# A graph network kernel: GpSimd waits for four gathers to land before it issues the next four

## The chip, the cores and the metric

The kernel runs on one core of a Trainium2 chip. The metric is the device time of one execution in microseconds, from the first to the last instruction and what lies around them; lower is better.

## The reference: what is computed

There are 6,250 nodes of 160 numbers (64 scalars, 32 vectors of three) and 206,250 edges, sorted by destination. Two layers follow each other, each with a residual and a layer norm:

```
layer 0:  message = (products of x[src] with weights, scaled by the edge's 4 numbers)
                    * sigmoid(edge_scalars @ W_rad.T + b_rad)
          x = layernorm(x + linear(x + segment_sum(message, dst)))
layer 1:  w   = silu(edge_scalars @ Wfc1) @ Wfc2
          mid = w * (linear(x)[src] combined with the edge's 4 numbers)
          x = layernorm(x + sc(x) + alpha * linear(segment_mean(mid, dst)))
```

The costly part of each layer is the same: fetch one row per edge from a table of node rows in HBM, weight it by the edge's numbers, and sum the rows of equal destination.

## The kernel before

**Tiles.** 128 edges are a tile, four tiles a supertile (512 edges), four supertiles a round. There are 404 supertiles, that is 101 rounds, in each layer. The node rows are multiplied by the weights once, ahead of the edges, and stored in HBM as `table0` (448 floats, 1,792 bytes a row) and `table1` (224 floats, 896 bytes a row).

**Gathers.** GpSimd (POOL) fetches rows with indirect DMAs, 128 rows each, so four for a supertile (`gather`, line 361): 1,616 in each layer. The rows of a supertile go to one of four slots, `rows0[:, j]` or `rows1[:, j]`, with j the supertile's place in its round. Each slot has a semaphore, `s_rows[l][j]`, which the DMA engines raise by 16 for each landed gather, so by 64 for a supertile. Before GpSimd issues the gathers of slot j again, it waits until ScalarE (`s_wtd`) and VectorE (`s_wone`) have read the rows of four supertiles ago, and at slot 0 also for the row numbers of this round (`s_src`, the buffer `srcs`). It never waits for its own gathers. The first 16 gathers of a layer are issued before the loop, with no wait between them.

**The other engines.** For each supertile of layer 0, ScalarE weights the rows by three of the edge's numbers (line 433) and takes the sigmoid (line 459). VectorE adds finished sums of two supertiles ago (line 668), weights by the fourth number (line 609), makes the one-hot matrices of the destinations (line 660), sums the parts (line 625) and makes the messages (line 632). TensorE makes the radial product of the supertile after the next (line 883) and the sums of this one (line 907). Layer 1 is alike: lines 433 and 517 on ScalarE, 668, 612, 660 and 645 to 655 on VectorE, 900, 892 and 907 on TensorE. The order is written out by hand, and each engine runs its own loop over the rounds.

**Loads by SP.** SyncE (SP) loads the edge scalars and destinations of two supertiles at a time into buffers that are used again each round, and after them the row numbers for the round after the next (line 270). That load is issued only when all gathers that used the buffer have landed.

Of the kernel before, what the change touches and what calls it, by code (L numbers as in the profile page):

```python
# [11 lines left out]
TPS = 4  # L12
SUP_EDGES = TPS * P
SLOTS = 4
# [33 lines left out]
def mk_gnn_resnorm_d2_gnn_r8_694f30_kernel(nc, a):  # L48
# [5 lines left out]
    with ctx:  # L54
# [3 lines left out]
        def sem(name):  # L58
            return ctx.enter_context(nc.semaphore(name))
# [117 lines left out]
        s_rows = [[sem(f"rows_gathered{l}_{j}") for j in range(SLOTS)] for l in range(2)]  # L177
        s_pool, s_sp = sem("pool_went_on"), sem("sp_went_on")
# [157 lines left out]
        @block.gpsimd  # L336
        def _(pool):
            pool.dma_start(dsts, a["dsts"]).then_inc(s_dsts, 16)
            for t, name in WEIGHTS:
                pool.dma_start(t[:], a[name]).then_inc(s_weights, 16)  # L340
            nc.gpsimd.memset(zeros[:], 0.0).then_inc(s_const, 1)
            nc.gpsimd.memset(eps[:], EPS).then_inc(s_eps, 1)
            nc.gpsimd.memset(ident[:], 0.0).then_inc(s_const, 1)
            pool.wait_ge(s_const, 2)
            nc.gpsimd.affine_select(out=ident[:], in_=ident[:], compare_op=ALU.not_equal, fill=1.0, base=0,
                                    pattern=[[-1, P]], channel_multiplier=1).then_inc(s_const, 1)
            nc.gpsimd.memset(msg0[:, :, :, DIM:MSG0], 1.0).then_inc(s_zero0, 1)
            nc.gpsimd.memset(acc0[:, :, DIM:MSG0], 0.0).then_inc(s_zero0, 1)

            pool.wait_ge(s_ends, 2)  # L350
            for e in range(2):
                pool.dma_start(wends_d[e:e + 1, :].rearrange("o (p s) -> (o p) s", s=SLOTS),
                               wends[:, e, :]).then_inc(s_endsout, 16)
            pool.wait_ge(s_endsout, 32)
            pool.dma_start(wtabf[:, 0:2, :], wends_d.rearrange("(o e) s -> o e s", o=1)).then_inc(s_endsin, 16)
            nc.gpsimd.iota(iota[:], pattern=[[1, NODES_PAD]], base=0, channel_multiplier=0).then_inc(s_const, 1)

            def gather(l, j, b):
                rows, table = (rows0, table0) if l == 0 else (rows1, table1)
                for t in range(TPS):  # L360
                    pool.indirect_dma_start(  # L361
                        out=rows[:, j, t, :], out_offset=None, in_=table,
                        in_offset=bass.IndirectOffsetOnAxis(ap=srcs[:, b, j, t:t + 1], axis=0)).then_inc(s_rows[l][j], 16)

            def gathers(l):
                pool.wait_ge(s_src[l][0], 16)
                for j in range(SLOTS):
                    gather(l, j, 0)

                def gathers_of_round(r, b, loads):  # L370
                    for j in range(SLOTS):
                        s = (r - 1) * SLOTS + j
                        pool.wait_ge(s_wtd[l], s + 1)
                        pool.sem_inc(s_pool, 1)
                        pool.wait_ge(s_wone[l], s + 1)
                        pool.sem_inc(s_pool, 1)
                        if j == 0:
                            pool.wait_ge(s_src[l][b], loads * 16)
                            pool.sem_inc(s_pool, 1)
                        gather(l, j, b)  # L380

                with pool.Fori(0, TWOS) as i:
                    gathers_of_round(i * 2 + 1, 1, i + 1)
                    gathers_of_round(i * 2 + 2, 0, i + 2)

            for j in range(GROUP):
                pool.wait_ge(s_tst[j], 16 * GROUPS)
            pool.wait_ge(s_wtab, 1)
            gathers(0)

            pool.wait_ge(s_done[0], 1)
            nc.gpsimd.memset(tails[:, NODE_TILES * MV:], 0.0).then_inc(s_tails, 1)
            nc.gpsimd.tensor_copy(tails[:, 0:NODE_TILES * MV].rearrange("p (w c) -> p w c", w=NODE_TILES),
                                  acc0[:, :, P:DIM]).then_inc(s_tails, 1)
            nc.gpsimd.memset(og_tail[:, :, GROUP * MV:], 0.0).then_inc(s_pad, 1)
            nc.gpsimd.memset(arena[:, 0:KEPT0], 0.0).then_inc(s_zero1, 1)
            nc.gpsimd.memset(arena[:, KEPT1:], 0.0).then_inc(s_zero1, 1)

            for g in range(GROUPS):
                pool.wait_ge(s_fev, (g + 1) * GROUP)  # L400
                pool.wait_ge(s_ln[0], (g + 1) * LN_STEPS[0])
                to, f = acc0[:, g * GROUP:(g + 1) * GROUP, :], feat[:, g % 2]
                nc.gpsimd.tensor_tensor(to[:, :, 0:P], f[:, :, 0:P], og[:, g % 2], ALU.add)
                nc.gpsimd.tensor_tensor(to[:, :, P:DIM], f[:, :, P + ROW1:],
                                        og_tail[:, g % 2, 0:GROUP * MV].rearrange("p (g c) -> p g c", g=GROUP),
                                        ALU.add).then_inc(s_base, 1)

            for b in range(2):
                pool.wait_ge(s_fst[b], (GROUPS + 1 - b) // 2 * 16)
            pool.wait_ge(s_base, GROUPS)  # L410
            gathers(1)
# [753 lines left out]
```

## Time and profile before

| what | us |
|---|---|
| median of 3 runs | 5922.7 |
| lowest and highest | 5918.03, 5962.53 |
| span of the profiled execution, first to last instruction | 5900.5 |
| busy: TensorE, VectorE, ScalarE, GpSimd | 3955.8, 3891.0, 3383.0, 3146.9 |

The list of times does not say which of them is the profiled execution; the lowest is 17.5 us above its span. A share of busy time is an average over the whole span. The indirect DMA's busy time on GpSimd is the time in which it writes the descriptors; the bytes move behind it, and where they do can be read from the share and rate of the DMA engines in short stretches. Layer 0 gathers from 66 us to 2860 us and layer 1 from 2993 us to 5801 us. The granted TensorE clock is 0.5 of full speed in most of layer 0 and mostly full in layer 1.

### The profile page before, as it was taken

What the parts mean: (1) busy time and instruction counts of PE and PEld (TensorE: products, weight loads), DVE (VectorE), ACT (ScalarE), POOL (GpSimd) and SP (SyncE); (2) the same over time, 40 slices, a digit from 0 to 9 for tenths busy, and PEclk for the clock granted to TensorE, in tenths of its full rate; (3) what the DMA queues carried; (4) which work ended last, traced back from release to release, by engine and by line L of the source; (5) the groups of instructions that cost most, each with busy time, mean ns of one, the idle gap of its engine ahead of it and who ended that gap; (6) DMA issues with size and microseconds to landing.
All of it is one profiled execution on the core that took longest, in us unless ns stands there. A gap on an engine that the chain in (4) does not pass through costs nothing.

```text
span 5900.5 us, 82997 instructions
## 1 busy us (share of the span) xinstructions
PE 3955.8 (67%) x16478; PEld 2613.9 (44%) x16479; DVE 3891.0 (66%) x12732; ACT 3383.0 (57%) x10841; POOL 3146.9 (53%) x3275
## 2 busy tenths in 40 slices
PE   5555555555565565565667777778777777777776
PEld 3444444444444444454544343434434334344345
DVE  4666666666666666666656666667666666666666
ACT  3556655655655565665555565555555555555554
POOL 4555555555555555555345555555555555555551
PEclk7555555555555555555688888888888888888888
DMA  7555555555555555555332222222222222222222
GB/s 232 140 142 143 141 145 139 141 144 139 141 145 140 138 146 139 139 145 142 90 81 75 74 75 74 78 73 77 75 74 75 73 72 75 73 76 77 74 76 53
DMA packets 325631, 641.98 MB, mean 109 GB/s; under 512 B 143598, under 2 KB 175131, under 8 KB 325499
## 3 DMA queue, kind: packets, MB, share of 16 engines
q0 software_dynamic: 181584, 557.89, 34.8%
q1 hardware_dynamic: 144016, 83.72, 5.4%
q8 instruction: 14, 0.23, 0.0%
q14 instruction: 17, 0.14, 0.0%
HBM read 620.47 MB, written 20.88 MB: 109 GB/s over the span
## 4 chain that ended last, share of the span: by engine, by line
DVE 34%; another core or an unknown queue 23%; PE 22%; issue 12%; DVEq 4%; ACT 3%; DMA 1%; POOL 0%; SPq 0%; ACTq 0%
PE ps L907 15%; DVE work L625 10%; DVE onehot L660 7%; DVE work L609 5%; ACT work L433 3%; PE ps L900 3%; DVE work L612 2%; PE ps L892 2%; DVEq L676 2%; DVE work L648 2%; DVE dstf L704 1%; DVEq L721 1%; DVE work L655 1%; DVE acc L668 1%
## 5 line engine op out<-in xcount | busy, mean ns | idle before, releaser
L361 POOL DMA_INDIRECT arena<-table,srcs x1616 | 1541.1, 954 | 1292.1 <-issue 486.4
L361 POOL DMA_INDIRECT work<-table,srcs x1616 | 1560.7, 966 | 1249.9 <-issue 435.9
L433 ACT ACTIVATE work<-arena,dst_sh 128x96 f32<-128x96 f32 (+1 forms) x4848 | 1416.3, 378 | 569.9 <-DVE arena L632 496.1
L907 PE MATMUL ps<-work,onehot 128*128 128x384 f32 x3616 | 1493.6, 564 | 176.7 <-DVE work L655 114.8
L433 ACT ACTIVATE work<-work,dst_sh 128x96 f32<-128x96 f32 (+1 forms) x4848 | 1499.1, 398 | 21.0 <-issue 11.0
L883 PE MATMUL ps<-wrad,escal 17*128 17x160 f32 x3232 | 561.7, 495 | 1195.2 <-DVE arena L632 1119.4
L907 PEld LDWEIGHTS ps<-work,onehot 128*128 128x128 f32 x3616 | 754.5, 218 | 842.8 <-issue 534.0
L907 PE MATMUL ps<-arena,onehot 128*128 128x161 f32 x3616 | 1077.2, 478 | 10.3 <-issue 7.5
L883 PEld LDWEIGHTS ps<-wrad,escal 17*128 17x128 f32 x3232 | 406.0, 309 | 1349.2 <-DVE arena L632 866.0
L907 PEld LDWEIGHTS ps<-arena,onehot 128*128 128x128 f32 x3616 | 921.4, 319 | 138.9 <-issue 128.0
L517 ACT ACTIVATE hid<-ps 128x256 f32<-128x256 f32 x404 | 152.2, 377 | 1197.6 <-remote 867.7
L660 DVE TENSOR_SCALAR onehot<-iota,dstf 128x128 f32 x3616 | 794.7, 291 | 16.3 <-issue 6.4
L900 PE MATMUL ps<-fc,hid 64*128 64x192 f32 x3232 | 423.4, 386 | 503.0 <-ACT hid L517 407.4
L668 DVE TENSOR_TENSOR arena<-arena,ps 128x384 f32 x455 | 250.8, 551 | 753.5 <-remote 537.3
L668 DVE TENSOR_TENSOR acc<-acc,ps 128x161 f32 x455 | 145.4, 319 | 816.9 <-remote 740.0
L625 DVE TENSOR_REDUCE work<-work 128x256 f32<-128x768 f32 (+1 forms) x808 | 657.0, 855 | 0.0
L900 PEld LDWEIGHTS ps<-fc,hid 64*128 64x128 f32 x3232 | 288.9, 209 | 752.3 <-ACT hid L517 481.3
L459 ACT ACTIVATE ps<-ps 128x640 f32<-128x640 f32 x404 | 276.1, 683 | 576.8 <-remote 569.7
L609 DVE SCALAR_TENSOR_TENSOR work<-arena,dst_sh,work 128x96 f32<-128x96 f32 x1616 | 405.7, 313 | 0.0
L652 DVE TENSOR_TENSOR work<-work,ps 128x768 f32<-128x768 f32 x404 | 382.5, 947 | 0.0
L632 DVE TENSOR_TENSOR arena<-work,ps 128x640 f32<-128x640 f32 x404 | 331.7, 821 | 14.0
L612 DVE TENSOR_SCALAR work<-work,dst_sh 128x96 f32<-128x96 f32 x1616 | 334.1, 281 | 5.7 <-DMA work<-table,srcs 5.7
(122 smaller groups left out, 2090.2 us busy)
## 6 DMA issues: line engine op xcount, KB each, us to landing
escal<-in_escal SPq DMA_DIRECT2D x404, 98.0 KB
arena<-table,srcs POOLq DMA_INDIRECT x1616
work<-table,srcs POOLq DMA_INDIRECT x1616
table<-work SPq DMA_DIRECT2D x49, 224.0 KB, 3.2
dst_sh<-in_dst_sh SPq DMA_DIRECT2D x404, 20.0 KB
table<-work SPq DMA_DIRECT2D x7, 784.0 KB, 4.0
acc<-in_xd SPq DMA_DIRECT2D x1, 3920.0 KB
arena<-in_xd SPq DMA_DIRECT2D x7, 560.0 KB, 4.2
```

The source lines that it names most:

```text
L361: pool.indirect_dma_start(out=rows[:, j, t, :], out_offset=None, in_=table, in_offset=bass.IndirectOffsetOnAxis(ap=srcs[:, b, j, t:t + 1], ...
L433: last = nc.scalar.activation(u[:, t, to:to + c1 - c0], r[:, t, c0:c1], ACT.Copy, scale=dst_sh[:, j, at:at + 1].bitcast(f32))
L609: last = nc.vector.scalar_tensor_tensor(to, rows0[:, j, t, 0:96], scale.bitcast(f32), to, ALU.mult, ALU.add)
L612: last = nc.vector.tensor_scalar(weighted1[:, j % 2, t, 448:544], rows1[:, j, t, 128:224], scale.bitcast(f32), None, ALU.mult)
L625: nc.vector.tensor_reduce(to, parts[:, :, :, 0:MS].rearrange("p t k c -> p t c k"), AX.X, ALU.add).then_inc(s_part[0], 1)
L632: nc.vector.tensor_tensor(m[:, :, 0:DIM], u[:, :, 0:DIM], c, ALU.mult).then_inc(s_msg[0], 1)
L652: nc.vector.tensor_tensor(blocks(m[:, :, 192:384], 3), blocks(u[:, :, 256:544], 3)[:, :, :, 0:MS], bc(w[:, :, 64:128], 2, [P, TPS, 3, MS]) ...
L660: last = nc.vector.tensor_scalar(onehot[:, b, t, :], iota[:, bass.ds(window * P, P)], dstf[:, j % 2, t:t + 1], None, ALU.is_equal)
L668: return nc.vector.tensor_tensor(to, to, bank(b)[:, 0:n], ALU.add)
L883: last = mm(rad[j % 2][:, t, :], escal[r, j, t % 2 * P:(t % 2 + 1) * P], wrad[r, :], start=True, stop=True)
L900: last = mm(wps[j % 2][:, t, :], hid[h, j % 2, t % 2 * P:(t % 2 + 1) * P], fc2[h, :], start=True, stop=True)
L907: last = mm(bank(to)[:, 0:(MSG0, MSG1)[l]], onehot[:, b, t, :], m[:, j % 2, t, :], start=t == 0, stop=t == TPS - 1)
```

## The change

In `gathers_of_round`, which issues the gathers of round r, a wait stands ahead of each supertile's four gathers: for the slot whose gathers were issued last (slot j - 1 of this round, or slot 3 of the round before). The `sem_inc` behind it is the pattern that already stands behind the other waits. Nothing else differs; the first 16 gathers of each layer are as before.

```
                         if j == 0:
                             pool.wait_ge(s_src[l][b], loads * 16)
                             pool.sem_inc(s_pool, 1)
+                        pool.wait_ge(s_rows[l][j - 1 if j else SLOTS - 1], (r + (j > 0)) * 16 * TPS)
+                        pool.sem_inc(s_pool, 1)
                         gather(l, j, b)
```

## Rows read from the trace of the kernel before

**Rows 1.** First and last gather of each layer: duration ns min/median/max, start us.

```profile
L361 POOL DMA_INDIRECT arena<-table,srcs x1616: 940/946/1086, 66.1 to 2860.0; - x180
L361 POOL DMA_INDIRECT work<-table,srcs x1616: 947/953/1172, 2993.4 to 5801.4; - x180
```

**Rows 2.** The page's costliest groups: busy us, mean ns | idle before, releaser.

```profile
L361 POOL DMA_INDIRECT arena<-table,srcs x1616 | 1541.1, 954 | 1292.1 <-issue 486.4
L361 POOL DMA_INDIRECT work<-table,srcs x1616 | 1560.7, 966 | 1249.9 <-issue 435.9
```

**Rows 3.** Who waited for whom: total us, times, longest us.

```profile
DVE acc L668 <- remote: 740.0, 102, 10.3
...
DVE arena L668 <- remote: 537.3, 88, 16.0
...
POOL arena L361 <- issue: 486.4, 1404, 38.2
...
POOL arena L361 <- DVE work L609: 405.7, 108, 8.5
...
POOL arena L361 <- DMA srcs<-in_srcs: 398.5, 99, 6.9
POOL work L361 <- DMA srcs<-in_srcs: 347.1, 95, 10.0
```

**Rows 4.** Timeline inside layer 0: start us, us, instruction, count, idle before.

```profile
1502.97 0.31 SPq L270 DMA_DIRECT2D srcs<-in_srcs  x1
...
1505.71 0.94 POOL L361 DMA_INDIRECT arena<-table,srcs  x1 [3.53 <-DMA srcs<-in_srcs]
...
1519.57 0.95 POOL L361 DMA_INDIRECT arena<-table,srcs  x1 [0.30 <-issue]
1522.99 0.33 DVE L668 TENSOR_TENSOR acc<-acc,ps 128x161 f32 x1 [7.49 <-remote]
1523.23 1.00 DVE L609 SCALAR_TENSOR_TENSOR work<-arena,dst_sh,work 128x96 f32<-128x96 f32 x4
...
1525.02 0.94 POOL L361 DMA_INDIRECT arena<-table,srcs  x1 [4.51 <-DVE work L609]
```

**Rows 5.** Stretches: length, busy of five engines, PEclk, DMA share, GB/s.

```profile
1522.25:1522.50 0.25, 0.00 (x0) 0.00 (x0) 0.00 (x0) 0.00 (x0) 0.00 (x0) 0.50 0.26 100
1522.50:1522.75 0.25, 0.00 (x0) 0.00 (x0) 0.00 (x0) 0.00 (x0) 0.00 (x0) 0.50 0.04 14
...
2999.25:2999.50 0.25, 0.00 (x0) 0.00 (x0) 0.00 (x0) 0.00 (x0) 0.13 (x1) 0.50 0.29 108
2999.50:2999.75 0.25, 0.00 (x0) 0.00 (x0) 0.00 (x0) 0.00 (x0) 0.07 (x1) 0.50 0.00 0
```

**Rows 6.** Timeline at the start of layer 1.

```profile
2997.18 0.95 POOL L361 DMA_INDIRECT work<-table,srcs  x1 [0.30 <-issue]
...
2999.90 3.72 ACT L433 ACTIVATE work<-work,dst_sh 128x96 f32<-128x96 f32 x12 [7.53 <-DMA work<-table,srcs]
```

**Rows 7.** The page's DMA issues: KB each, median us to landing.

```profile
srcs<-in_srcs SPq DMA_DIRECT2D x202, 8.0 KB, 1.7
```

**Rows 8.** Stretches of layers 0 and 1, columns as in group 5.

```profile
100.00:2860.00 2760.00, 1589.89 (x6763) 1310.74 (x6761) 1852.14 (x5419) 1639.92 (x5181) 1520.44 (x1595) 0.53 0.52 142
3000.00:5802.00 2802.00, 2130.15 (x8379) 1118.37 (x8380) 1839.91 (x6645) 1596.33 (x5221) 1555.20 (x1611) 0.84 0.29 75
```

**Rows 9.** Timeline inside layer 1, TensorE's products of one supertile.

```profile
4400.24 5.49 PE L907 MATMUL ps<-work,onehot 128*128 128x384 f32 x8 [1.46 <-DVE work L655]
...
4407.38 2.85 PE L907 MATMUL ps<-work,onehot 128*128 128x384 f32 x8
...
4419.79 1.65 PE L900 MATMUL ps<-fc,hid 64*128 64x192 f32 x8 [5.36 <-ACT hid L517]
4421.38 1.11 PE L892 MATMUL ps<-escal,wfc 16*64 16x256 f32 x4
```

More of the change, by code:

```diff
@@ L379, in gathers_of_round @@
                             pool.sem_inc(s_pool, 1)
+                        pool.wait_ge(s_rows[l][j - 1 if j else SLOTS - 1], (r + (j > 0)) * 16 * TPS)
+                        pool.sem_inc(s_pool, 1)
                         gather(l, j, b)
```

## The prediction

> **What bounds the kernel now.** I read the extent of the gathers first, then the waits, then one round of the timeline, then short stretches of the DMA engines. In layer 0 the first and the last of 1,616 gathers start at 66.1 and 2860.0 us [rows 1], so a supertile of four takes (2860.0 - 66.1) / 1615 x 4 = 6.92 us; in layer 1 (5801.4 - 2993.4) / 1615 x 4 = 6.955 us. The two layers are 5,602 of the span's 5,900 us, so what the change does to the pace of a supertile is what it does to the time.
>
> The reader is to see that nobody is busy for the whole of those 6.9 us. VectorE, the busiest of the others in layer 0, works 1852 us for about 399 supertiles, 4.6 us each, and 1840 us in layer 1, again 4.6 [rows 8]. GpSimd needs four descriptor writings and the three 0.30 us gaps between them: 4 x 0.954 + 0.9 = 4.72 us in layer 0, 4 x 0.966 + 0.9 = 4.76 in layer 1 [rows 2, 4]. So it stands idle ahead of a group for 6.92 - 4.72 = 2.20 us on average, and 6.955 - 4.76 = 2.195 in layer 1. This mean hides two kinds. Of 1,616 gathers of layer 0, 1,404 follow with no wait but issue; 1,212 of them are inside a group, so 192 groups, nearly half, come straight behind the group before. The other half waits 3.8 to 4 us, 99 times for the row numbers and 108 times for VectorE [rows 3]. One round looks like that: a wait for `srcs`, three or four groups in a row up to 1520.52, then a wait for line 609 [rows 4].
>
> Why VectorE is late is odd. At line 668 it waits 740 us in 102 pieces in layer 0 and 537 us in layer 1 for something that the profile cannot name ("remote") [rows 3]. In the piece shown it stands from 1515.5 to 1522.99 [rows 4], and the last gather's bytes stop between 1522.50 and 1522.75 [rows 5]: the stall ends when the gathers have drained. The trace doesn't say whether one causes the other.
>
> **What the change costs.** It removes nothing and moves nothing. It adds 400 waits and 400 semaphore increments on GpSimd in each layer; the increments themselves are of the kind that stands there thrice already and lie inside idle time. Queued behind the new wait are only the next four gathers: GpSimd does nothing else in the loop. Who waits for those are ScalarE (line 433), VectorE (609 or 612) and SP (line 270). The new idle time ahead of a group is the time from the end of the fourth descriptor writing to the landing, plus the time GpSimd takes to start once the semaphore is up.
>
> *Landing.* In layer 0 the group's last writing ends at 1519.57 + 0.95 = 1520.52 [rows 4]; the DMA share is 0.26 in the quarter before 1522.50 and 0.04 in the next [rows 5]: bytes end about 2.2 us behind the writing (bounds 2.0 and 2.25). In layer 1, with rows of half the size, it ends at 2998.13 [rows 6], and the DMA engines are at 0.29 up to 2999.50 and at 0 behind it [rows 5]: about 1.4 us. ScalarE, which waits for just that landing, starts at 2999.90 [rows 6], so at most 0.4 us lies between the last byte and a visible semaphore with the start of ScalarE. The Trainium skill, "DMA: Bandwidth & Descriptors", section on the anatomy of one DMA on the gpsimd path, puts the fixed cost of a DMA at about 2.0 us and most of it behind the last byte, until the write is confirmed. The 0.4 us of layer 1 speaks against such a tail here. By the page some 1.5 us would come on top in each layer, and the time would be 6437 + 2 x 400 x 1.5 = 7637 us.
>
> *Start of GpSimd.* No row shows GpSimd waiting for gathers; the nearest are its waits for two others. VectorE's line 609 ends at 1524.23, GpSimd starts at 1525.02: 0.79 us. SP issues `srcs` at 1502.97, it lands 1.7 us later in the median [rows 7], 1504.67, and GpSimd starts at 1505.71: 1.04 us [rows 4]. The second is the same kind, a DMA's semaphore, so I take 1.04. The ends of the range are 0.30, the gap with no wait at all, and 1.3.
>
> *Sum.* Layer 0: 4.72 + 2.2 + 1.04 = 7.96 us a supertile against 6.92: +1.04. Layer 1: 4.76 + 1.4 + 1.04 = 7.20 against 6.955: +0.245. Over 400 groups in each layer: 416 + 98 = +514 us. Now the gathers follow one another in a chain without a break, and GpSimd sets the pace. What waits before, the row numbers and VectorE, falls inside: with 4.6 us of work for 8.0 or 7.2, the others wait for rows, and have read a slot three groups before GpSimd wants it; `srcs` is asked for at the start of the round before, some 25 us ahead. Even if all of the unnamed stall stays (740 / 101 = 7.3 us a round in layer 0), the others need 4 x 4.6 + 7.3 = 25.7 us, and the chain takes 31.8. What is late next is therefore the rows themselves, at line 433 and 612. The sum is made against the profiled span, 5900.5 + 514 = 6414.5; the median of the runs stands 22.2 above that span, so the forecast is 5922.7 + 514 = **6437 us**.
>
> **The rivals.**
> *Added, not instead (0.14).* If the two old waits of a round stay, because VectorE is held by the stall whatever GpSimd does, only the two groups that now come back to back pay: 2.2 + 1.04 - 0.3 = 2.9 us each in layer 0, 2.1 in layer 1, so (5.9 + 4.3) x 100 = +1,020 us and 6940 us. For it speaks that the stall's cause is unknown; against it that its work plus stall fit into the chain.
>
> *TensorE's low clock (0.09, most of it in part).* In layer 1 TensorE's products of a supertile take 5.49 + 1.65 + 1.11 = 8.25 us at the lower of its two levels (1.2 GHz), where line 907 alone falls to 2.85 at the higher [rows 9]. If it stood at the low level through layer 1, it would be the bound: (8.25 - 6.955) x 400 = +518 in layer 1 instead of +98, 6857 us. Against it: granted clock 0.84 there now, with TensorE busy 76% [rows 8], and an engine at 8.25 of 7.20 has no gap left. In layer 0 the clock is 0.53 already and TensorE busy 1590 of 2760 us, so it costs nothing there. The Trainium skill, "TensorE: Matmul & The Clock Gate", says that the throttled state is the default and activity releases it; by that rule a TensorE that is always busy would leave the low level, so the price is a part of this.
>
> *A late landing (0.04).* The tail behind the last byte that no row of layer 0 excludes: 7637 us as worked out above, from the point where it is over 0.4 us.
>
> *Not slower (0.05).* One mechanism: GpSimd starts on a raised semaphore as fast as it goes on without one, 0.30 us. Then the idle time ahead of a group is 2.5 us in layer 0 and 1.7 in layer 1, against 2.20 and 2.195 now: (0.3 - 0.5) x 400 = -80 us, 5843 us, since the shorter bursts would let the unnamed stalls go. It decides at a start of 0.40 us: the two gaps must add up to less than 4.395, and the landings alone are 3.6. ScalarE's start within 0.4 speaks for it, both rows of GpSimd (0.79, 1.04) against. That the change does nothing (the wait always met, within 1%) would need the landing inside the old gaps: impossible for the 192 groups that start 0.30 us behind the last, so I give it 0.01.
>
> **Numbers.** The forecast's case has 0.67. Its own range comes from the bounds of the terms: with 0.79 and landings of 2.0 and 1.35, (0.59 + -0.055) x 400 = +214, 6137; with 1.3, 2.25 and 1.5, (1.35 + 0.605) x 400 = +782, 6705. Both ends at once are unlikely; 6300 to 6580 holds most of it. To leave out no more than two in ten, the range reaches up into the rivals in part: 6270 to 6730. A measurement of this kernel tells about 1% from no change. Faster by over 1%: 0.03. Within 1%: 0.03. Slower by over 1%: 0.94.
>
> **What the profile after would show.** Right: every group of four gathers stands 3.1 to 3.4 us (layer 0) and 2.3 to 2.6 us (layer 1) behind the one before, released by a gather's landing; first to last gather take about 3,210 and 2,905 us; the waits for `srcs` and line 609 are gone; the "remote" waits are gone or turned into waits for rows. Wrong: long gaps of two kinds as before (added, not instead); line 907 near 5.5 us for eight products through layer 1 (clock); a gap over 4 us although the DMA engines are at rest (late landing); gaps near 2.5 and 1.7 (not slower). The weakest term is the start of GpSimd: each 0.1 us of it is 80 us.

## The result and the profile after

| | median us | lowest, highest | runs |
|---|---|---|---|
| before | 5934.42 | 5918.03, 5962.53 | 4 |
| changed | 6486.2 | 6484.39, 6489.43 | 4 |

The changed kernel takes 1.0936 times as long, 95% interval 1.0895 to 1.0977: +552 us by the medians. The forecast was 6437 us, +514. The profiled execution has a span of 6482.6 us against 5900.5, +582. The profiled execution of the changed kernel is listed at 6484.39, 1.8 us above its span, so of the 22.2 us that the forecast put on top for the kernel before, about 20 are spread between its executions. In the new profile every line of the kernel behind line 380 has a number higher by two: 609 is 611, 668 is 670, 907 is 909.

First the extent of the gathers, which answers to [rows 1] (count, then duration ns min/median/max, first and last start us):

```profile
L361 POOL DMA_INDIRECT arena<-table,srcs x1616: 940/946/1067, 66.5 to 3307.1; - x180
L361 POOL DMA_INDIRECT work<-table,srcs x1616: 947/953/1172, 3434.2 to 6383.6; - x180
```

A supertile takes (3307.1 - 66.5) / 1615 x 4 = 8.026 us in layer 0, against 6.920, and 7.305 in layer 1, against 6.955. Over 404 supertiles that is +447 and +141 us; the stretch between the layers shrinks from 133.4 to 127.1. 447 + 141 - 6 = 582 is the whole difference of the spans.

The page's groups answer to [rows 2] (busy us, mean ns | idle before, main releaser):

```profile
L361 POOL DMA_INDIRECT arena<-table,srcs x1616 | 1529.2, 946 | 1751.9 <-DMA arena<-table,srcs 1312.4
...
L361 POOL DMA_INDIRECT work<-table,srcs x1616 | 1544.6, 956 | 1407.2 <-DMA work<-table,srcs 1009.0
```

The releaser is now the landing of gathers. Who waited for whom, as in [rows 3] (total us, times, longest):

```profile
POOL arena L361 <- DMA arena<-table,srcs: 1312.4, 399, 6.1
...
DVE work L611 <- ACT work L435: 1075.9, 395, 4.9
...
POOL work L361 <- DMA work<-table,srcs: 1009.0, 400, 3.3
POOL arena L361 <- issue: 438.9, 1215, 39.5
...
POOL work L361 <- issue: 390.0, 1193, 2.0
```

399 waits of 3.29 us in the mean, 400 of 2.52: one for each of the 400 groups behind a layer's first four, but for one in layer 0. No "remote" wait is left among the listed ones, and none of GpSimd's for `srcs`. VectorE waits for ScalarE (line 435), and ScalarE for rows. The profile names the rows in only 201 of ScalarE's waits at line 435 and puts 601 down to "issue", but in the kernel ScalarE waits there for the same semaphore as GpSimd, and it starts about 0.7 us ahead of GpSimd each time. The chain of waits that ended last says the same at a glance; before, it was 34% VectorE, 23% unnamed and 22% TensorE:

```profile
DMA 35%; issue 29%; POOL 23%; PE 3%; DVE 3%; ACT 2%; POOLq 1%; DVEq 0%; ACTq 0%
DMA arena<-table,srcs 20%; DMA work<-table,srcs 15%; POOL arena L361 12%; POOL work L361 11%; PE ps L909 2%; ACT work L435 2%; PE ps L1085 0%; DVE work L792 0%; DVE work L614 0%; POOLq L373 0%; ACT arena L480 0%; DVE acc L831 0%; DVE onehot L662 0%; DVE arena L670 0%; DVE work L650 0%
```

One group in the timeline of layer 0, then one of layer 1 (start, duration, instruction, count, idle before):

```profile
1503.97 0.95 POOL L361 DMA_INDIRECT arena<-table,srcs  x1 [0.30 <-issue]
...
1507.53 3.51 ACT L435 ACTIVATE work<-arena,dst_sh 128x160 f32<-128x160 f32 x12 [3.92 <-issue]
1508.24 0.94 POOL L361 DMA_INDIRECT arena<-table,srcs  x1 [3.32 <-DMA arena<-table,srcs]
```

```profile
4405.95 0.96 POOL L361 DMA_INDIRECT work<-table,srcs  x1 [0.31 <-issue]
...
4408.72 0.81 DVE L614 TENSOR_SCALAR work<-work,dst_sh 128x96 f32<-128x96 f32 x4 [0.65 <-DMA work<-table,srcs]
...
4409.47 0.95 POOL L361 DMA_INDIRECT work<-table,srcs  x1 [2.56 <-DMA work<-table,srcs]
```

And the quarter microseconds in which the bytes of these two groups end (columns as in [rows 5]):

```profile
1506.75:1507.00 0.25, 0.25 (x4) 0.03 (x2) 0.00 (x0) 0.00 (x0) 0.00 (x0) 0.50 0.20 79
1507.00:1507.25 0.25, 0.25 (x3) 0.14 (x1) 0.00 (x0) 0.00 (x0) 0.00 (x0) 0.50 0.00 0
...
4408.00:4408.25 0.25, 0.25 (x4) 0.19 (x4) 0.06 (x1) 0.00 (x0) 0.00 (x0) 1.00 0.37 126
4408.25:4408.50 0.25, 0.25 (x4) 0.00 (x0) 0.00 (x0) 0.00 (x0) 0.00 (x0) 1.00 0.00 0
```

In layer 0 the fourth writing ends at 1504.92 and the bytes end between 1506.75 and 1507.00, 1.8 to 2.1 us later. The first engine that waits for them, ScalarE, starts at 1507.53, and GpSimd at 1508.24, another 0.71 us behind. In layer 1 the writing ends at 4406.91, the bytes between 4408.00 and 4408.25 (1.1 to 1.3 us), VectorE starts at 4408.72 and GpSimd at 4409.47.

One more kind of gap stands in this profile, inside a group and with no landing before it:

```profile
1542.83 0.94 POOL L361 DMA_INDIRECT arena<-table,srcs  x1 [2.05 <-issue]
```

It is 2.05 us where its neighbours are 0.30, and it comes back after every 104 gathers, 15 times in each layer. Its cause isn't known.

### The profile page after: what moved, and what is told of

Same layout as the page of the kernel before. It is cut to its first block, busy times and chain, and to the rows that moved or that the text cites. A ratio compares the mean times of both kernels' runs of the same rounds, so it can differ in the third digit from the quotient of the medians.

```text
span 6482.6 us, 84097 instructions
## 1 busy us (share of the span) xinstructions
PE 4113.2 (63%) x16478; PEld 2679.2 (41%) x16479; DVE 3993.6 (62%) x12732; ACT 3378.2 (52%) x10841; POOL 3118.6 (48%) x3275
## 4 chain that ended last, share of the span: by engine, by line
DMA 35%; issue 29%; POOL 23%; PE 3%; DVE 3%; ACT 2%; POOLq 1%; DVEq 0%; ACTq 0%
DMA arena<-table,srcs 20%; DMA work<-table,srcs 15%; POOL arena L361 12%; POOL work L361 11%; PE ps L909 2%; ACT work L435 2%; PE ps L1085 0%; DVE work L792 0%; DVE work L614 0%; POOLq L373 0%; ACT arena L480 0%; DVE acc L831 0%; DVE onehot L662 0%; DVE arena L670 0%; DVE work L650 0%
## 5 line engine op out<-in xcount | busy, mean ns | idle before, releaser
L361 POOL DMA_INDIRECT work<-table,srcs x1616 | 1544.6, 956 | 1407.2 <-DMA work<-table,srcs 1009.0
L909 PE MATMUL ps<-work,onehot 128*128 128x384 f32 x3616 | 1657.8, 617 | 293.9 <-issue 197.4
L909 PEld LDWEIGHTS ps<-work,onehot 128*128 128x128 f32 x3616 | 829.2, 240 | 1039.2 <-issue 691.2
L909 PE MATMUL ps<-arena,onehot 128*128 128x161 f32 x3616 | 1091.6, 483 | 11.6 <-DVE arena L634 7.1
L662 DVE TENSOR_SCALAR onehot<-iota,dstf 128x128 f32 x3616 | 823.3, 299 | 16.3 <-DVE arena L670 8.1
L902 PE MATMUL ps<-fc,hid 64*128 64x192 f32 x3232 | 395.0, 365 | 380.7 <-ACT hid L519 355.4
L647 DVE TENSOR_TENSOR half<-work 128x128 f32<-128x128 f32 x404 | 118.0, 292 | 732.7 <-ACT work L435 669.4
L902 PEld LDWEIGHTS ps<-fc,hid 64*128 64x128 f32 x3232 | 269.4, 196 | 649.9 <-ACT hid L519 558.4
L894 PE MATMUL ps<-escal,wfc 16*64 16x256 f32 x1616 | 285.0, 431 | 0.0
```

Of the source, the lines that this page charges most:

```text
L361: pool.indirect_dma_start(out=rows[:, j, t, :], out_offset=None, in_=table, in_offset=bass.IndirectOffsetOnAxis(ap=srcs[:, b, j, t:t + 1], ...
L662: last = nc.vector.tensor_scalar(onehot[:, b, t, :], iota[:, bass.ds(window * P, P)], dstf[:, j % 2, t:t + 1], None, ALU.is_equal)
L894: last = mm(hps[h * HID:(h + 1) * HID, 0:2 * P], wfc1[r, :], escal[r, j, :], start=True, stop=True)
L902: last = mm(wps[j % 2][:, t, :], hid[h, j % 2, t % 2 * P:(t % 2 + 1) * P], fc2[h, :], start=True, stop=True)
L909: last = mm(bank(to)[:, 0:(MSG0, MSG1)[l]], onehot[:, b, t, :], m[:, j % 2, t, :], start=t == 0, stop=t == TPS - 1)
```

## The experiments

Two theories stood at the start. **The chain:** the pace of a supertile is the descriptor writing plus landing plus GpSimd's start, and nothing else of the kernel counts any more. **The stall:** the old unnamed waits at line 668 come from gathers issued without a break, so that a part of the wait's price is given back by their going, and a shorter break could beat both kernels.

The first runs showed something that neither had foreseen. Each kernel is timed beside the kernel before on the same chip, and **on three chips of four the kernel before takes 4391 us, not 5934.** So an expectation that adds to 5934 stands on a base that most of these chips don't have. All ratios below are against the kernel before on the same chip; the chips are called quick (4391 us) and stalling (5,920 to 6,020 us).

| run | chip | this us | before us | ratio, 95% interval |
|---|---|---|---|---|
| e1_layer0 | quick | 5590.71 | 4391.77 | 1.2737, 1.2716 to 1.2758 |
| e2_two_back | quick | 4390.0 | 4391.77 | 0.9999, 0.9989 to 1.0008 |
| e3_every_second | quick | 5522.36 | 4391.77 | 1.2586, 1.2565 to 1.2607 |
| e4_ahead1 | quick | 5553.89 | 4391.77 | 1.2654, 1.2633 to 1.2675 |
| e5_before_again | quick | 4390.2 | 4391.26 | 0.9997, 0.9986 to 1.0007 |
| e6_after_again | quick | 6483.32 | 4391.26 | 1.4759, 1.4734 to 1.4783 |
| e7_half_rows | quick | 6177.04 | 4391.26 | 1.4066, 1.4038 to 1.4094 |
| e8_ahead2 | quick | 4591.22 | 4391.26 | 1.0452, 1.0435 to 1.0470 |
| e9_once_a_round | stalling | 6033.12 | 6021.36 | 1.0009, 0.9985 to 1.0034 |
| e10_ahead2_again | stalling | 5879.71 | 5920.47 | 0.9925, 0.9902 to 0.9948 |
| e11_every_second_again | stalling | 5502.69 | 5920.47 | 0.9302, 0.9271 to 0.9333 |
| e12_short_break | quick | 5108.0 | 4391.06 | 1.1632, 1.1598 to 1.1666 |

### The wait in layer 0 alone

```
+                        if l == 0:
+                            pool.wait_ge(s_rows[l][j - 1 if j else SLOTS - 1], (r + (j > 0)) * 16 * TPS)
+                            pool.sem_inc(s_pool, 1)
```

> The new wait stands in layer 0 alone. Both theories: if the cost is the exposed landing and start, group by group, layer 0 pays what it pays in the changed kernel, (8.026 - 6.920) x 404 = +447 us, and layer 1 keeps 6.955 us a supertile: 5934 + 447 = 6381 us. If the two layers are coupled (clock, loads), layer 1 comes out away from 6.955 and the total by more than 40 us from 6381.

Its time was off by the base alone, as its gathers show:

```profile
L361 POOL DMA_INDIRECT arena<-table,srcs x1616: 940/946/1037, 66.2 to 3307.5; - x180
L361 POOL DMA_INDIRECT work<-table,srcs x1616: 949/953/1105, 3434.8 to 5491.2; - x180
```

Layer 0 has 8.028 us a supertile, the changed kernel's pace to within 0.002, though this chip is a quick one. Layer 1, without the wait, has 5.093, where the first profile of the kernel before had 6.955. So the wait in layer 0 leaves layer 1 alone (the kernel before has 5.089 there on a quick chip, below), and the price in layer 0 on a quick chip is 5590.7 - 4391.8 = +1199 us.

### The kernel before, and the changed one, once more on a quick chip

Both are unchanged.

> The kernel before, unchanged. In the first comparison it took 5934 us, in the second, beside the first four experiments, 4392. Theory C, the unnamed stall belongs to the chip (or its condition) that runs the kernel: here it takes either about 4392 or about 5930, in all its runs the same, and its profile at 4392 shows no unnamed waits of VectorE and groups 5.06 us apart, at 5930 such waits of over 400 us a layer. Theory S, the kernel has two paces of its own between which it falls by chance: runs of both kinds stand side by side.

> The changed kernel, unchanged. Its chain of descriptor writing, landing and start has nothing to do with the stall: 6486 us within 20, on whichever kind of chip. Against a kernel before of 4392 that is a ratio of 1.477, against 5930 one of 1.094. Rival, the chip of the second comparison is faster at gathers as such: then the gap ahead of a group is under 3.27 us and the time below 6400.

The profile of the kernel before on this chip: the extent of its gathers, and its two stretches with the columns of [rows 8].

```profile
L361 POOL DMA_INDIRECT arena<-table,srcs x1616: 942/947/1068, 66.0 to 2107.5; - x180
L361 POOL DMA_INDIRECT work<-table,srcs x1616: 949/954/1107, 2235.3 to 4289.7; - x180
```

```profile
100.00:2100.00 2000.00, 1550.96 (x6764) 1280.18 (x6763) 1835.70 (x5421) 1629.01 (x5174) 1514.33 (x1589) 0.55 0.71 195
2300.00:4290.00 1990.00, 1828.52 (x8213) 974.77 (x8211) 1791.84 (x6498) 1568.40 (x5089) 1513.36 (x1565) 0.98 0.39 102
```

A supertile takes 5.056 and 5.089 us: four descriptor writings of 0.95 to 0.97 us and four gaps of 0.30. Here GpSimd, writing descriptors without a pause, sets the pace itself. VectorE is busy 1835.70 of 2000 us, nearly as much. In the first profile both did nearly the same work [rows 8] and the span was 5900.5 - 4388.7 = 1,512 us longer: nearly all of that was waiting. In its waits "remote" is no longer among the long ones, and that for `srcs`, 398.5 us in [rows 3], is 8.8:

```profile
POOL arena L361 <- issue: 492.0, 1492, 37.6
...
POOL arena L361 <- DMA srcs<-in_srcs: 8.8, 23, 2.1
```

The changed kernel takes 6483 us here and took 6486 in the first comparison: it is the same everywhere. What differs is what it replaces. On a quick chip the wait costs 6483.3 - 4391.3 = +2092 us.

### Waiting for the group two back

```
+                        pool.wait_ge(s_rows[l][(j - 2) % SLOTS], (r + (j > 1)) * 16 * TPS)
+                        pool.sem_inc(s_pool, 1)
```

> The same number of waits and increments, but for the group before the last. Theory exposed landing: the group two back has landed long ago (about 2.2 us behind its last descriptor, while the next group takes 4.7 us to issue), so nothing waits: 5934 within 30 us, with the waits for srcs, line 609 and the unnamed releaser as before. Rival, the wait and its increment cost by themselves: about 0.1 us or more a supertile, 5934 + 80 or more; a tenth of a microsecond is the gap of two instructions in the queue.

The same wait and the same increment, with one group always in flight, costs nothing. Its waits:

```profile
POOL arena L361 <- DMA arena<-table,srcs: 81.3, 267, 0.3
```

Each of these is 0.30 us, the gap with no wait. So neither instruction has a price of its own; the price of the change is the empty queue. (Expected were 5934 us, the old base again; "as the kernel before" is what held.)

### Every second group, on both kinds of chip

```
+                        if j % 2 == 0:
+                            pool.wait_ge(s_rows[l][j - 1 if j else SLOTS - 1], (r + (j > 0)) * 16 * TPS)
+                            pool.sem_inc(s_pool, 1)
```

> The wait stands at slots 0 and 2 only, so two groups follow back to back and the third waits for a landing. Theory A, VectorE's unnamed stall comes from long unbroken rows of gathers and ends where they drain: rows of eight are short enough, and GpSimd sets the pace at (8.03 + 5.02) / 2 = 6.52 us a supertile in layer 0 and (7.31 + 5.06) / 2 = 6.18 in layer 1, 5934 - 162 - 311 = 5460 us, faster than before. Theory B, the stall comes whatever GpSimd does and the changed kernel only had room for it: the round stays at 27.7 us or grows by the added landing of slot 2, 2.9 us in layer 0 and 2.2 in layer 1: 5934 to 6450 us, with the unnamed waits still over 400 us a layer.

> The kernel of e3 once more, for the same reason. Beside a kernel before of 4390: 5522 again. Beside one of 5930 to 6030: theory A, with breaks of 3.3 and 2.5 us after every eight gathers the unnamed stalls are gone and GpSimd sets the pace, 5522 us, faster than the kernel before; theory B, they stay and the time is 5900 or more.

On the quick chip 5522 us and on the stalling one 5503, for the same kernel. One is 26% slower than the kernel before beside it, the other 7% faster. The first expectation's 5460 us was near because it counts the chain alone; "faster than before" failed on the quick chip. The gathers of layer 0 on the stalling chip, then GpSimd's waits for the landing and the largest unnamed ones:

```profile
L361 POOL DMA_INDIRECT arena<-table,srcs x1616: 943/949/1187, 66.0 to 2748.8; - x180
```

```profile
POOL arena L361 <- DMA arena<-table,srcs: 677.2, 199, 4.3
POOL work L361 <- DMA work<-table,srcs: 501.0, 199, 3.0
...
ACT hid L520 <- remote: 394.5, 164, 7.1
DVE arena L671 <- remote: 152.5, 51, 5.9
DVE acc L671 <- remote: 141.3, 38, 5.5
```

The pace is 6.645 us in layer 0, against 6.667 on the quick chip: what unnamed waits remain lie inside the chain. A break in every eight gathers, of 677.2 / 199 = 3.4 us in layer 0 and 2.5 in layer 1, is enough to take the stall off the path. On the quick chip the same kernel gives the breaks themselves, ahead of slot 0 and then of slot 2:

```profile
1508.14 0.94 POOL L361 DMA_INDIRECT arena<-table,srcs  x1 [3.22 <-DMA arena<-table,srcs]
...
1521.52 0.94 POOL L361 DMA_INDIRECT arena<-table,srcs  x1 [3.69 <-DMA arena<-table,srcs]
```

### The same wait later in the group

In these the wait for the group before stands inside `gather`, ahead of the second gather of the four (`t == 1`, e4_ahead1, shown) or of the third (`t == 2`, e8_ahead2 and e10_ahead2_again):

```
                 for t in range(TPS):
+                    if t == 1 and r is not None:
+                        pool.wait_ge(s_rows[l][j - 1 if j else SLOTS - 1], (r + (j > 0)) * 16 * TPS)
+                        pool.sem_inc(s_pool, 1)
```

> GpSimd issues the first gather of a group at once and waits for the group before ahead of the second, so one descriptor writing lies inside the landing. Exposed landing: the chain of a group is 3.27 us (landing and start, as measured in the changed kernel) plus three gathers without the last gap, 3.45 us: 6.72 us in layer 0, 2.51 + 3.47 = 5.98 in layer 1. Theory A (the stall comes from long rows): nothing else binds, 5934 - 0.20 x 404 - 0.975 x 404 = 5460 us. Theory B (it comes anyway): the others need about 27 us a round, no faster than 5850, and slower than 5934 if the waits add up.

> Two gathers of a group go out at once, the wait stands ahead of the third. The chain of a group is 3.27 + 1.25 + 0.95 = 5.47 us in layer 0, and in layer 1 the 2.51 us are shorter than the two gathers that lie in them (2 x 1.25 + 0.3 = 2.8), so the wait is met: 5.06. If only the chain counts: 4392 + (5.47 - 5.06) x 404 = 4558 us, which is faster than a stalled kernel before (5930) and 4% slower than an unstalled one (4392). If the unnamed stall comes back with rows of gathers this dense, on a chip that has it, 5500 to 5930.

> The kernel of e8 once more, to see it on a chip of the stalling kind. If the kernel before beside it takes about 4390, it takes 4591 again and nothing new is learned. If the kernel before takes 5930 to 6030: theory A (the unnamed stalls need rows of gathers with hardly a break) would have them gone or few, and the time under 5000 us; theory B (on such a chip they come with gathers at this density, whatever waits stand between) leaves unnamed waits of over 400 us a layer and 5500 to 6000 us.

Each gather issued ahead of the wait hides about its own 1.25 us of the landing. In the order wait at once, one ahead, two ahead, layer 0 takes 8.03, 6.86 and 5.54 us a supertile (steps of 1.17 and 1.32), and 5.06 with no wait in effect. Gathers of e4_ahead1, then of e8_ahead2:

```profile
L364 POOL DMA_INDIRECT arena<-table,srcs x1616: 940/946/1058, 66.9 to 2835.8; - x180
L364 POOL DMA_INDIRECT work<-table,srcs x1616: 947/953/1242, 2963.6 to 5452.6; - x180
```

```profile
L364 POOL DMA_INDIRECT arena<-table,srcs x1616: 940/946/1071, 67.4 to 2305.0; - x180
L364 POOL DMA_INDIRECT work<-table,srcs x1616: 947/953/1117, 2432.9 to 4494.9; - x180
```

Both times came out above the chain's sum (5554 us for 5460, 4591 for 4558). In e4_ahead1 the gap that comes once in 104 gathers falls on the break and makes it 4.4 to 5.1 us in layer 0 and 3.7 to 4.4 in layer 1; 30 of them are some 80 of the 94 us. One of layer 0:

```profile
1509.69 0.95 POOL L364 DMA_INDIRECT arena<-table,srcs  x1 [4.94 <-issue]
```

With the wait ahead of the third, layer 1 is at 5.107, as good as free.

On the stalling chip the kernel with the wait ahead of the third is not saved by its short breaks: 5880 us, 0.75% below the kernel before beside it, and the old picture stands again (theory B of its expectation, where e11_every_second_again bore out theory A):

```profile
DVE acc L671 <- remote: 652.6, 110, 10.3
...
DVE arena L671 <- remote: 505.2, 91, 16.0
...
POOL arena L364 <- DMA srcs<-in_srcs: 413.5, 98, 5.9
```

### One wait in a round of sixteen gathers

```
+                        if j == 0:
+                            pool.wait_ge(s_rows[l][SLOTS - 1], r * 16 * TPS)
+                            pool.sem_inc(s_pool, 1)
```

> The wait stands at slot 0 alone, so each round is a row of 16 gathers and a break until they have landed: the pattern of the kernel before in the first comparison (break at slot 0 for srcs, then a row), put on purpose. Theory S (the kernel falls into the slow pace once its gathers come in such rows): unnamed waits of VectorE appear and the round takes 27 to 28 us, about 5930. Theory C (the unnamed waits belong to the chip or its condition in the first comparison, and the pattern is their effect): only the chain counts, (8.03 + 3 x 5.06) / 4 = 5.80 us in layer 0 and (7.31 + 3 x 5.06) / 4 = 5.62 in layer 1, 4391 + (0.74 + 0.56) x 404 = 4916 us, if the kernel before beside it takes 4391 again. If the kernel before beside it takes about 5930, the chip is of the other kind, and the unnamed waits should stand in this profile too.

Here the kernel before takes 6021 us, so the chip is a stalling one, and this kernel takes 6033: no difference. Its unnamed waits at line 671 are 823.1 us in 106 pieces in layer 0, as large as in [rows 3]. One break in a round does not remove one stall in a round. But on such a chip the kernel before has that break already, waiting for `srcs` at slot 0; this kernel still has 406.2 us of that wait in 99 pieces in layer 0, so the new wait changed next to nothing, and the run doesn't show what a break does where there was none. And the kernel before shows the long time in all nine of its runs beside this one, and on the quick chips in none, so what makes the difference is the chip or its condition, and not the program.

### Half rows in layer 0

```
+                rows, table = (rows0, table0.rearrange("n (h c) -> (n h) c", h=2)) if l == 0 else (rows1, table1)
...
+                        out=rows[:, j, t, 0:ROW1], out_offset=None, in_=table,
```

> The changed kernel whose layer 0 gathers fetch 896 bytes a row instead of 1792 (the first half of a row; the other half is left at zero, so layer 0 leaves half of the rows out). If the landing's 2.15 us are bytes in part and the start of GpSimd about 1.1 us whatever the size, the gap ahead of a group falls from 3.27 to layer 1's 2.51 us and the time by 0.76 x 404 = 307 us, to 6180 (plus some 10 us for clearing the other halves once). If the landing is a fixed time, it stays at 6486.

The edit reads the table as twice as many rows of 896 bytes and leaves the row numbers as they are. So halves of rows are fetched, but mostly not of the right ones, and all lie in the first half of the table. Measured 6177.04 us (6176.18 to 6177.9). Its gathers in layer 0, and the waits of both layers:

```profile
L362 POOL DMA_INDIRECT arena<-table,srcs x1616: 940/946/1043, 68.6 to 2997.3; - x180
```

```profile
POOL work L362 <- DMA work<-table,srcs: 1007.1, 399, 3.3
POOL arena L362 <- DMA arena<-table,srcs: 1004.9, 400, 3.0
```

Layer 0 falls from 8.03 to 7.254 us, and its break from 3.29 to 2.51 us, exactly that of layer 1 (2.52), whose rows have this size. So the 0.77 us between the layers come with the row's size, and the other 2.5 us are there whichever of the two sizes the rows have. That the region read is half as large too, as in layer 1, isn't separated from the size of a row.

### A short break in every eight gathers

If such a break cures the stalling chip and costs the quick one 26%, a shorter one might do both. This has the wait of `t == 1` at even slots alone:

```
+                    if t == 1 and r is not None and j % 2 == 0:
```

> Between e3 and e8: at slots 0 and 2 the first gather goes out at once and the wait stands ahead of the second, so after every nine gathers there is a break of 3.27 - 0.3 - 0.95 = about 2 us in layer 0 and 1.3 in layer 1. By the chain: (6.72 + 5.06) / 2 = 5.89 us a supertile in layer 0, (5.98 + 5.06) / 2 = 5.52 in layer 1, 4391 + 0.83 x 404 + 0.46 x 404 = 4912 us beside a kernel before of 4391. Beside one of about 5920 (a chip of the stalling kind): if breaks of this length are enough to keep the stalls inside the pace, 4900 to 5200 us, better there than e3's 5503; if not, unnamed waits of over 400 us a layer and 5700 to 5950.

A miss: 5108 us where 4912 were expected, 16% slower than the kernel before on a quick chip, so no version for both. Its waits:

```profile
POOL arena L364 <- DMA arena<-table,srcs: 456.8, 184, 3.5
...
POOL work L364 <- DMA work<-table,srcs: 251.3, 184, 2.2
```

These are 184 of the 200 breaks in a layer. Who waited for the gathers counts the rest in, which the profile puts down to "issue":

```profile
POOL arena L364: 533.4, 199
POOL work L364: 312.4, 200
```

So the mean break in layer 0 is 533.4 / 199 = 2.68 us where I had 2.0, from the kernel that waits in every group (there four gathers follow one another between breaks, here eight), and in layer 1 it is 1.56 for the 1.3 I had: 0.68 x 200 + 0.26 x 200 = 188 of the 196 us. Two things are in it. The 184 breaks are 456.8 / 184 = 2.48 us in layer 0 and 251.3 / 184 = 1.37 in layer 1, so after eight gathers in a row the awaited one can land later than after four. In the kernel with the wait in every second group it does so at one slot of the two, 3.69 us ahead of slot 2 against 3.22 ahead of slot 0 in the rows above. And the gap that comes once in 104 gathers falls on a break here too and makes it 4.6 to 5.8 us in layer 0 and 3.7 to 4.3 in layer 1, 15 times in each. Whether a backlog of bytes or SP's loads hold the landing wasn't separated. Whether this kernel frees a stalling chip wasn't tried.

No kernel tried beats the one before on a quick chip. On the stalling chip the best of the three tried there is the wait in every second group, 5503 us, which is also less than the changed kernel's 6483 to 6486, wherever that ran.

## Why the prediction was right, and where it was thin

**The mechanism held point by point.** A supertile is four writings, three gaps, one landing and one start, and each term can now be read:

| us | layer 0 forecast | measured | layer 1 forecast | measured |
|---|---|---|---|---|
| four writings | 3.82 | 3.78 | 3.86 | 3.82 |
| three gaps | 0.90 | 0.99 | 0.90 | 0.98 |
| landing and start | 3.24 | 3.29 | 2.44 | 2.52 |
| sum | 7.96 | 8.06 | 7.20 | 7.32 |
| by first and last gather | | 8.026 | | 7.305 |

The measured gaps are GpSimd's waits for issue: (438.9 - 39.5) / 1214 = 0.33 us and 390.0 / 1193 = 0.33, where I took 0.30 for all. The 68 us by which the span's +582 exceeds +514 are (0.066 + 0.105) x 400. Most of them are a term that the sum didn't have: 30 gaps of 2.05 us for 0.30 are 30 x 1.75 = 53 us.

**Two errors inside "landing and start" nearly cancelled.** The landings, to the last byte, were 2.2 and 1.4 and measured at most 2.08 and 1.34, in the one group of each layer read here. The start was 1.04; from the last byte to GpSimd's next writing it is at least 1508.24 - 1507.00 = 1.24 and 4409.47 - 4408.25 = 1.22 us. I had let the landing end at the last byte and the start begin at the semaphore, so the time between the two was in neither term. I had bounded it by 0.4 us through ScalarE, and that reading was wrong: the bytes end somewhere between 2999.25 and 2999.50 [rows 5] and ScalarE starts at 2999.90 [rows 6], so 0.40 us is the least that lies between them, and 0.65 the most. By the same row the landing of layer 1 was 1.12 to 1.37 us, not 1.4. That the sum of the two terms came out within 0.05 and 0.08 us is in part luck.

**What was late before went inside the chain**, as the prediction said: no waits for `srcs` or for line 609 of GpSimd's that count, and no listed "remote". What is late next is the rows, at lines 435 and 614.

**The rivals.** *Added, not instead* (6940): there is one kind of gap ahead of a group, not two. *The low clock* (6857): the stretch of layer 1 gives

```profile
3400.00:6300.00 2900.00, 2243.17 (x8334) 1161.05 (x8333) 1885.37 (x6549) 1579.59 (x5140) 1507.91 (x1575) 0.84 0.27 71
```

a granted clock of 0.84, unchanged, with TensorE busy 77%: its worst case was never reached. On the quick chip the kernel before had 0.98 in this layer and the changed one 0.83, so part of the clock is lost under the change there, but not on the path. *A late landing* (7637): 0.53 to 0.78 us lies between the last byte and ScalarE's start in layer 0, 0.47 to 0.72 before VectorE's in layer 1. The Trainium skill, "DMA: Bandwidth & Descriptors", section on the anatomy of one DMA, puts most of a 2.0 us fixed cost behind the last byte, and calls HBM the slowest target; these gathers write to SBUF. The trace does not agree: 0.8 us is the most that can be there, the start of ScalarE or VectorE included. It is more than the 0.4 us at which the prediction let this rival begin, but 1.5 us on top would have made breaks of 4.7 and 3.9 us where 3.29 and 2.52 were measured. *Not slower* (5843): it needed a start below 0.40, and from the last byte it is at least 1.22.

**What the prediction didn't see** is that its base was not one number. It took 6.92 us a supertile, 2.2 of it idle, as a property of the kernel; it called the stall odd and left its cause open, which was fair, but it did not ask what the kernel would take without it. GpSimd's own work, 4.72 us plus one gap of 0.30, is 5.02, and 5.056 is what it takes on a quick chip. Had the comparison run there, the same sum for the changed kernel (7.96 x 404 + 7.20 x 404 and what lies around) would have stood against 4391, and +514 would have been +2092. The time of the changed kernel was predicted; its ratio was predicted for one kind of chip.

**Open:** what the stall is. Not the rate of the gathers alone, since quick chips run them back to back through both layers without it. Not the program, which is the same. Whether it is the chip itself, or something else that ran on it at the time, no run separates. In the first profile the stall ends with the gathers: of VectorE's 98 unnamed waits of over 3 us at line 668 in layer 0, 79 end 2.2 to 2.8 us behind the last descriptor writing, and of the 72 in layer 1, 60 end 2.1 to 2.4 us behind it. GpSimd by then waits for VectorE, so each of the two holds the other, and which one begins isn't shown. That breaks of 3.4 and 2.5 us in eight gathers keep the stall off the path is measured on one chip only. So is that short ones in four do not: they are 0.6 to 1.2 us by slot in layer 0 on the quick chip, and in layer 1 there are hardly any (5.107 against 5.089 us a supertile), so for layer 1 short breaks weren't tried.

## What to carry to other kernels

A wait that empties GpSimd's own DMA queue costs the landing and the start every time (here 3.3 and 2.5 us in each group), whatever else is idle; the same wait with one group left in flight cost nothing on the quick chip. Ahead of pricing a change against idle time, work out what the kernel would take if that idle time were not there, and when its releaser has no name, run the unchanged kernel on more than one chip. A break that pays on a chip with a stall of its own (0.930) can cost 26% on one without.

## What the runs showed of the hardware

**One program, two times, by chip.** 4391 us on three chips, 5,920 to 6,020 on a fourth, and 5934 in the first comparison. On the fourth chip two comparisons gave 6021 and 5920; within each, the kernel before stayed within 0.6%. The difference shows as "remote" waits: by the profile, which models the ends of TensorE's products, TensorE's results are there and the engines that wait for them go on much later. The kernel before, first profile, TensorE's product and VectorE's line 668 that uses it:

```profile
1538.73 2.52 PE L907 MATMUL ps<-arena,onehot 128*128 128x161 f32 x8
```

```profile
1550.52 0.69 ACT L459 ACTIVATE ps<-ps 128x640 f32<-128x640 f32 x1 [3.82 <-remote]
1550.56 0.32 DVE L668 TENSOR_TENSOR acc<-acc,ps 128x161 f32 x1 [8.71 <-remote]
```

```profile
1550.25:1550.50 0.25, 0.00 (x0) 0.00 (x0) 0.00 (x0) 0.00 (x0) 0.00 (x0) 0.50 0.00 0
```

The product ends at 1541.25, and VectorE, idle since 1541.85, starts at 1550.56. ScalarE, which waits for another product of TensorE, goes on at 1550.52, and the DMA engines have been at rest since 1550.25 at the latest. In the profiles from the quick chips no such wait is among the long ones.

**GpSimd starts later than others on the same landing.** ScalarE 1507.53 and GpSimd 1508.24; VectorE 4408.72 and GpSimd 4409.47: 0.71 and 0.75 us. In the changed kernel it is so throughout: 0.70 to 0.86 us behind ScalarE in some 400 groups of each layer. A part of it may be the 0.30 us that stand between two of its writings even with no wait; the runs don't separate the two.

**The writing of a gather's descriptors doesn't depend on the row's bytes:** median 946 ns for full and for half rows.

**One gap in 104 gathers is long where GpSimd waits in its loop.** In the changed kernel it is 2.05 us, 15 times in each layer. With the wait in layer 0 alone, layer 1 has no gap longer than 0.3 us put down to issue:

```profile
POOL work L361 <- issue: 456.8, 1499, 0.3
```

Nor has the kernel before on a quick chip (1,523 gaps in layer 1, the longest 0.3 us).
